# Centring on GpSimd and a constant row in place of the bias products, in a thirty-step recurrence

## What is computed

```python
def step(h, _):
    h = h + 0.01 * jnp.tanh(h)
    h = h * jax.nn.sigmoid(h)
    h = _layernorm(h, ln_w, ln_b)
    h = jnp.einsum('bsc,dc->bsd', h, W) + b
    return (h, None)
x, _ = jax.lax.scan(step, x, None, length=N_ITERS)   # N_ITERS = 30
...
x = x + _L1_ffn_ref(_layernorm(x, axis=-1), L1_ffn_ln_w, L1_ffn_ln_b, L1_ffn_W, L1_ffn_b)
```

## Time and profile before

| | us |
|---|---|
| median of 3 runs | 1304.41 (1303.4 to 1305.09) |
| the profiled execution's own time | 1303.05 |
| its span, first to last instruction | 1301.1 |
| PE, DVE, ACT, POOL busy | 1269.5, 1163.0, 961.4, 755.8 |
| granted TensorE clock, mean | 0.997 |

### The profile page before, as it was taken

One profiled execution on the slowest core, in us unless ns is written; L12 is line 12 of the kernel. 1 busy time (PEld: TensorE's weight loads), 2 busy tenths in 40 slices (PEclk: granted clock), 3 DMA queues, 4 the chain that ended last, 5 costly groups with the idle time before them and its releaser, 6 DMA issues.

```text
span 1301.1 us, 30193 instructions
## 1 busy us (share of the span) xinstructions
PE 1269.5 (98%) x9788; PEld 1150.9 (88%) x9788; DVE 1163.0 (89%) x3032; ACT 961.4 (74%) x1169; POOL 755.8 (58%) x787
## 2 busy tenths in 40 slices
PE   8899999999999999699999999999999999999998
PEld 7677777777777777599999999999999999999998
DVE  7888888888888877899999999999999999999996
ACT  2455555555555555799999999999999999999994
POOL 3455555455555554666666666666666666666664
PEclk9999999999999999899999999999999999999999
DMA  6111111111111000000000000000000000000004
GB/s 191 41 42 46 58 55 44 40 40 40 40 40 40 0 1 1 1 2 1 0 0 0 0 0 0 0 0 0 0 0 0 0 0 0 0 0 0 0 0 129
DMA packets 29810, 27.74 MB, mean 21 GB/s; under 512 B 3285, under 2 KB 21464, under 8 KB 29656
## 3 DMA queue, kind: packets, MB, share of 16 engines
q1 hardware_dynamic: 29784, 27.41, 6.6%
HBM read 23.21 MB, written 4.19 MB: 21 GB/s over the span
## 4 chain that ended last, share of the span: by engine, by line
PE 83%; DVE 10%; ACT 3%; issue 2%; POOL 0%; DMA 0%; SPq 0%; DVEq 0%; ACTq 0%
PE psum L867 33%; PE psum L909 16%; PE psum L884 8%; PE psum L652 4%; PE psum L654 4%; PE psum L653 4%; PE psum L823 4%; PE psum L674 3%; PE psum L669 3%; DVE emb_n L1465 2%; DVE xh_mem L1253 1%; PE psum L663 1%; ACT emb_f L1017 1%; PE psum L683 1%; DVE upd L1431 1%
## 5 line engine op out<-in xcount | busy, mean ns | idle before, releaser
L511 POOL TENSOR_TENSOR h_ring<-g_ring,f_rs 128x512 f32<-128x512 f32 x480 | 485.9, 1043 | 256.7 <-DVE f_rs L1358 256.6
L867 PE MATMUL psum<-w_t,y_all 128*128 128x128 f32 x3840 | 467.6, 275 | 0.0
L867 PEld LDWEIGHTS psum<-w_t,y_all 128*128 128x128 f32 x3840 | 448.0, 192 | 0.0
L1270 DVE BATCH_NORM_STATS2 f_stat<-g_ring 128x6 f32<-128x256 f32 x960 | 393.3, 423 | 2.4 <-ACT g_ring L966 2.4
L909 PE MATMUL psum<-ident,h_ring 128*128 128x128 f32 x1920 | 359.5, 273 | 3.2 <-POOL h_ring L511 2.8
L1287 DVE SCALAR_TENSOR_TENSOR u_ring<-t_ring,psum 128x1024 f32<-128x1024 f32 x232 | 283.3, 1221 | 32.3 <-ACT t_ring L976 27.7
L976 ACT ACTIVATE t_ring<-psum 128x1024 f32<-128x1024 f32 x232 | 238.0, 1026 | 53.7 <-PE psum L867 49.6
L909 PEld LDWEIGHTS psum<-ident,h_ring 128*128 128x128 f32 x1920 | 251.4, 142 | 15.8 <-POOL h_ring L511 3.6
L884 PE MATMUL psum<-bias,ones_bf 65*128 65x256 bf16 x960 | 262.1, 274 | 1.1 <-DVE u_ring L1287 1.1
L980 ACT ACTIVATE y_all<-psum 128x1024 f32<-128x1024 f32 x240 | 243.6, 1015 | 14.6 <-PE psum L909 14.6
L966 ACT ACTIVATE g_ring<-u_ring 128x1024 f32<-128x1024 f32 x240 | 251.6, 1049 | 1.9 <-DVE u_ring L1287 1.6
(11 more groups left out here) (191 smaller groups left out, 1990.5 us busy)
## 6 DMA issues: line engine op xcount, KB each, us to landing
work<-in_adj_dram SPq DMA_DIRECT2D x16, 1024.0 KB, 5.4
x_tok<-in_x_dram SPq DMA_DIRECT2D x16, 256.0 KB, 5.6
out_dram<-y_all SPq DMA_DIRECT2D x7, 512.0 KB, 3.2
work<-in_L_gnn_conv_w_dram SPq DMA_DIRECT2D x1, 1088.0 KB
out_dram<-y_all SPq DMA_DIRECT2D x2, 256.0 KB, 3.3
work<-in_L_gnn_w_ih_dram SPq DMA_DIRECT2D x1, 384.0 KB
work<-in_L_gnn_w_hh_dram SPq DMA_DIRECT2D x1, 192.0 KB
work<-in_L_gnn_W_dram SPq DMA_DIRECT2D x1, 64.0 KB, 5.2
```

The lines of the kernel that those rows point to most:

```text
L511: pool.tensor_tensor(tiles(h_ring[j % 4])[:, NT * h:NT * h + NT, :], tiles(g_ring[j])[:, NT * h:NT * h + NT, :], spread(f_rs[:, both(j), a ...
L867: m = pe.matmul(y_ps[k % 2][:, h, C * t:C * t + C], y_all[:, GT * k + NT * h + t, :], w1_t[:], start=False, stop=True, skip_group_check=True)
L1270: ins = dve.bn_stats(f_stat[:, j % 4, 0, 2 * q:2 * q + 2, :].rearrange("p t w -> p (t w)"), two)
```

## The change

The turned tiles get 127 rows of channels and a last row that holds 1, and the product's weight gets the bias in that row. For this the tiles have to be centred (their channels then sum to zero, so the last channel can be expressed by the others), which POOL does in the instruction that scales.

- POOL: `scale` issues eight tensor-scalars of 128x128 for a group in place of two multiplies of 128x512, each adding `f_less` (minus the mean) and multiplying by `f_rs`. `less_mean` makes `f_less` for two groups in one tensor-scalar of 128x16, in every second slot, after the statistics of both (`f_bn`), and announces it by `f_mean`, for which `scale` waits.
- PE: no `bias` and `bias_free`. The product starts its own accumulation (`start=(t == 0)`), and now waits at its start for the sum that frees `y_ps`. The turns write 127 partitions. `ones_row` fills each of the three banks of `g_ps` with 1, once, before its first turns; the turns leave the last partition alone, so its 1 stays.
- DVE: `split_bias` goes, with 17 instructions; in `fold` the weight's last column is subtracted from the others and replaced by the folded bias. `f_stat` holds eight groups instead of four.

```diff
+LAG_M = 4
...
+            def less_mean(j, s):
+
+                pool.wait_ge(f_bn, s + 2)
+                settle(pool, s_passed_pool)
+                pool.tensor_scalar(f_less[:, j:j + 2, :], f_stat[:, j:j + 2, 0, :, 1], -1.0, 1.0,
+                                   ALU.mult, ALU.mult).then_inc(f_mean, 1)
+
             def scale(i, j, s):
...
+                pool.wait_ge(f_mean, i * (GROUPS // 2) + j // 2 + 1)
                 wait(pool, f_turn, s - 3)
+                settle(pool, s_passed_pool)
                 for h in (j % 2, 1 - j % 2):
-                    at = GT * (j % 2) + NT * h
-                    pool.tensor_tensor(tiles(h_ring[j % 4])[:, NT * h:NT * h + NT, :], tiles(g_ring[j])[:, NT * h:NT * h + NT, :],
-                                       spread(f_rs[:, both(j), at:at + NT], NT, C), ALU.mult).then_inc(f_norm, 1)
+                    for t in range(NT * h, NT * h + NT):
+                        at = GT * (j % 2) + t
+                        ins = pool.tensor_scalar(tiles(h_ring[j % 4])[:, t, :], tiles(g_ring[j])[:, t, :],
+                                                 f_less[:, j, t:t + 1], f_rs[:, both(j), at:at + 1], ALU.add, ALU.mult)
+                    ins.then_inc(f_norm, 1)
...
             def product_group(it, k):
                 s = (it - 1) * GROUPS + k
                 pe.wait_ge(f_state, s + 1)
+                if ends(it, 1) and k < 2:
+                    pe.wait_ge(s_x3, B)
+                elif ends(it, ITERS) and k > 1:
+                    pe.wait_ge(f_out, k - 1)
+                else:
+                    pe.wait_ge(f_u, s + GROUPS - 1)
                 for h in range(2):
                     for t in range(NT):
-                        m = pe.matmul(y_ps[k % 2][:, h, C * t:C * t + C], y_all[:, GT * k + NT * h + t, :], w1_t[:],
-                                      start=False, stop=True, skip_group_check=True)
+                        m = pe.matmul(y_ps[k % 2][:, h, C * t:C * t + C], y_all[:, GT * k + NT * h + t, :], w1c_t[:],
+                                      start=(t == 0), stop=True, skip_group_check=True)
...
-            def bias(k, part):
-                h, c = part // 2, part % 2
-                pe.matmul(y_ps[(k + 1) % 2][:, h, 2 * C * c:2 * C * c + 2 * C], ones_bf[:],
-                          bias1[:, 0:2, :].rearrange("p t c -> p (t c)"),
-                          start=(c == 0), stop=False, skip_group_check=True)
+            def ones_row(b):
+
+                pe.matmul(bank[b], ones_bf[:], first_one[:], start=True, stop=True, skip_group_check=True)
...
-                        m = pe.transpose(g_ps[j % 2][:, t // NT, P * (t % NT):P * (t % NT) + P],
-                                         tiles(h_ring[j % 4])[:, t, :], ident[:])
...
+                    m = pe.transpose(g_ps[j % 2][0:P - 1, t // NT, P * (t % NT):P * (t % NT) + P],
+                                     tiles(h_ring[j % 4])[:, t, 0:P - 1], ident[:])
...
-                for r in range(3):
-                    dve.tensor_copy(b1_cols[:, 32 * r:32 * r + 1], vec(FB1))
+                link(dve.tensor_copy(vec(BF), w1_nat[:, C - 1:C]))
+                dve.tensor_scalar(w1_nat[:, 0:C - 1], w1_nat[:, 0:C - 1], vec(BF), None, ALU.subtract)
+                dve.tensor_copy(w1_nat[:, C - 1:C], vec(FB1))
...
-            def split_bias():
...
-                if isinstance(b, int) and b == 0:
-                    split_bias()
```

More of the change, by code:

```diff
@@ L102, in build @@
         y_all = sb("y_all", [P, B * NT, C])
-        w1_t = sb("w1_t", [P, C])
+        w1c_t = sb("w1c_t", [P, C])
         ident = sb("ident", [P, P])
         ones_bf = sb("ones_bf", [KB, P], BF16)
-        bias1 = sb("bias1", [KB, NT, C], BF16)
+        first_one = sb("first_one", [KB, N], BF16)
         half_neg = sb("half_neg", [P, 8])
-        f_stat = sb("f_stat", [P, 4, 2, GT, 3])
+        f_stat = sb("f_stat", [P, GROUPS, 2, GT, 3])
         f_var = sb("f_var", [P, BY_POWER, GT])
         f_rs = sb("f_rs", [P, 2, PAIR])
+        f_less = sb("f_less", [P, GROUPS, GT])
         f_share = sb("f_share", [P, PAIR])
@@ L297, in build @@
         f_bn = sem("f_bn")
+        f_mean = sem("f_mean")
         f_v = sem("f_v")
@@ L507, in scale @@
                     pool.wait_ge(f_root, pairs(i, j) + 1)
+                pool.wait_ge(f_mean, i * (GROUPS // 2) + j // 2 + 1)
                 wait(pool, f_turn, s - 3)
+                settle(pool, s_passed_pool)
                 for h in (j % 2, 1 - j % 2):
-                    at = GT * (j % 2) + NT * h
-                    pool.tensor_tensor(tiles(h_ring[j % 4])[:, NT * h:NT * h + NT, :], tiles(g_ring[j])[:, NT * h:NT * h + NT, :],
-                                       spread(f_rs[:, both(j), at:at + NT], NT, C), ALU.mult).then_inc(f_norm, 1)
+                    for t in range(NT * h, NT * h + NT):
[3 more added lines that the diff above has]
+                    ins.then_inc(f_norm, 1)
             def slot(it, k):
+                older = earlier(it, k, LAG_M)
+                if older is not None and k % 2 == 0:
+                    less_mean(*older[1:])
                 before = earlier(it, k, LAG_P)
@@ L561, in step @@
                     power(3)
+                    less_mean(2, 2)
                 if l1:
@@ L573, in step @@
                     power(0)
+                    less_mean(0, 0)
                     scale(0, 0, 0)
@@ L608, in spread_vectors @@
                 pe.wait_ge(s_folded1, 1)
-                pe.matmul(bank[TURN_A][0:KB, 0:C], b1_cols, ident[:], start=True, stop=True)
                 for j in range(8):
@@ L891, in slot @@
                 before = earlier(it, k, LAG_T)
[L892 to L899, removed]
-                for n in range(GT):
[L901 to L908, removed]
-                        m = pe.transpose(g_ps[j % 2][:, t // NT, P * (t % NT):P * (t % NT) + P],
-                                         tiles(h_ring[j % 4])[:, t, :], ident[:])
[L911 to L916, removed]
+                if before is None:
+                    return
+                i, j, s = before
+                if ends(i, 0) and j == 0:
+                    pe.wait_ge(s_conv_pre, B)
+                    ones_row(CONV)
+                    pe.wait_ge(s_x_nmp_lo, B)
+                    ones_row(CHAN)
+                elif ends(i, 0) and j == 1:
+                    pe.wait_ge(s_r, B)
+                    ones_row(DIST_A)
+                else:
+                    pe.wait_ge(f_state, s - 1)
+                pe.wait_ge(f_norm, 2 * s + 1)
+                for n in range(GT):
+                    if n == NT:
+                        pe.wait_ge(f_norm, 2 * s + 2)
+                        wait(pe, f_state, s)
+                    t = (n + NT * (j % 2)) % GT
+                    m = pe.transpose(g_ps[j % 2][0:P - 1, t // NT, P * (t % NT):P * (t % NT) + P],
+                                     tiles(h_ring[j % 4])[:, t, 0:P - 1], ident[:])
+                m.then_inc(f_turn, 1)
             slots(pe, slot, LAG_T, 2)
@@ L942, in weights_high @@
                 act.wait_ge(s_wturn, FILLS)
-                act.activation(w1_t[:], bank[CONV + (FILLS - 1) % 4][:, 0:C], ACT.Copy)
+                act.activation(w1c_t[:], bank[CONV + (FILLS - 1) % 4][:, 0:C], ACT.Copy)
                 act.activation(w_full[:, MSG, :], bank[CONV + (FILLS - 1) % 4][:, C:2 * C], ACT.Copy).then_inc(s_whigh, 1)
@@ L1269, in statistics_of @@
                 two = g_ring[j][:, 2 * C * q:2 * C * q + 2 * C].rearrange("p (o c) -> p c o", o=2)
-                ins = dve.bn_stats(f_stat[:, j % 4, 0, 2 * q:2 * q + 2, :].rearrange("p t w -> p (t w)"), two)
+                ins = dve.bn_stats(f_stat[:, j, 0, 2 * q:2 * q + 2, :].rearrange("p t w -> p (t w)"), two)
                 if q == GT // 2 - 1:
@@ L1308, in variance @@
                 dve.wait_ge(f_bn, j + 1)
-                squares = f_stat[:, j % 4, :, :, 2].rearrange("p o t -> p t o")
+                squares = f_stat[:, j, :, :, 2].rearrange("p o t -> p t o")
                 dve.tensor_reduce(f_var[:, j, :], squares, AX_X, ALU.add).then_inc(f_v, 1)
@@ L1338, in root_link @@
                         dve.wait_ge(s_z, B)
-                    squares = f_stat[:, j % 4:j % 4 + 2, :, :, 2].rearrange("p g o t -> p g t o")
+                    squares = f_stat[:, j:j + 2, :, :, 2].rearrange("p g o t -> p g t o")
                     dve.tensor_reduce(root[:, VAR, :].rearrange("p (g t) -> p g t", t=GT), squares, AX_X, ALU.add).then_inc(f_link, 1)
```

26 lines of the change are left out of this document (4 added, 22 removed).

## The result

The changed kernel is slower: 1404.07 us median of four runs (1403.82 to 1404.85) against 1303.91 for the kernel before on the same chip, a ratio of 1.0768 with a 95% interval of 1.075 to 1.0787. The forecast was 1267 us, with a range up to 1335.

What follows compares the result with a forecast made beforehand. PE was taken to bound the kernel at 3.110 us a slot, DVE next at 2.968. Loop -32.9, setup -1.3, loop start +0.5, last eight slots -3.0 sum to -36.7: 1266.3, as median 1267 us; range 1258 to 1335.

Steps and rivals of the forecast that it cites:

- PE's part: PE in the loop: without four bias records a slot takes 24 x 0.111 = 2.67 us, 0.44 less.
- the moved wait: PE, wait for the sum of the group before last, now ahead of the product: priced at 0 us.
- DVE binds next: Steady loop: DVE at 2.968 us stops PE's gain, 0.142 us a slot over 232 slots, 32.9 us.
- POOL's price: POOL's scaling: 0.30 us a tensor-scalar of 128x128, 5.0 us a pair of groups, which fits in 5.94.
- upper bound of 0.42: POOL's 128x128 tensor-scalar: at most 0.42 us start to start, from multiplies with two full inputs at 2.2 ns an element.
- The rival that POOL becomes the bound: POOL between f_root and f_norm: at 0.41 us a piece, slot 3.38 us, +64 us, 1366 us; chance 0.20.
- "In time": POOL's halves before PE's turns: each ready in time, the tightest by 0.2 us, with 0.30 us of PE idle behind.
- Setup: Before the loop: bias splitting goes, so at most PE's 1.34 us wait for emb_n goes, -1.3 us.
- Start of the loop: PE's wait for POOL's first half: four pieces, the small instruction and DVE's two-input sums cost +0.5 us.
- Last eight slots: End of the loop, PE sets the pace: eight times 0.44 is 3.5 us, taken as 3.0 saved.
- The port: Between DVE and POOL: contention taken as 0 in the loop, since DVE's inputs there include at most one from SBUF.
- The clock: PE's granted clock: under 1.00 would show the prediction wrong; 10% of short gaps were expected.

Runs made afterwards that it cites:

- the wide tensor-scalar: The changed kernel with one POOL tensor-scalar of 128x512 with two constants in place of four pieces of 128x128; 1253.26 us.
- the mixed kernels: Against the kernel before, POOL centres at most four tiles of a group; the others keep one multiply and bias products; 1274.60 to 1291.62 us.
- the run of 1686 us: The changed kernel, its tensor-scalars with one operation and one factor from memory (multiply by f_rs), mean not subtracted; 1686.28 us.

## Why the prediction was wrong, step by step

- **PE's part: right.** 24 records a slot at 0.111 us, turns of 127 columns included, as the rows of the wide tensor-scalar (1253 us) show. That the moved wait costs nothing is shown down to DVE's slot of 2.91 us, by that run and the one without bias products (1254 us), and no further.
- **DVE binds next: right, its size a little off.** The step took DVE's busy time of the kernel before, 2.968 us a slot, and allowed for some 0.03 of stalls in it. With the tanh ready in time it is 0.08 less, 2.888, and the slot 2.910. Where no wait is left, DVE's sum starts before its last statistics end (901.66 against 900.98 + 0.77 = 901.75 in the rows of the run without bias products), and its mean length is 1208 ns instead of 1221. The forecast of 1267 for a POOL that keeps up was 13 us too high.
- **POOL's price: the step that failed.** 0.30 us was assumed, 0.431 measured, above even the upper bound of 0.42. The slope behind it was right (the affine select over the small tensor-scalar gives (292 - 184) / 124 = 0.87 ns an element; 0.88 and 0.92 measured). Wrong was the fixed part: I took the length of one lone instruction, 292 ns, as if successive ones overlapped by 0.04 us. In a stream the next begins 0.065 us after the end: 0.362 in place of 0.25. The factors from memory then add 0.07, where 0.05 was allowed. The 0.04 came from long multiplies, and didn't hold for short pieces.
- **The rival that POOL becomes the bound: the mechanism and its formula were right.** 8 x 0.431 + 0.1 = 3.55 us a slot, 3.533 measured, and +0.44 x 236 = 104 in place of the prediction's 64 makes its 1366 into 1406. Its chance, 0.20, was too small, and the range stopped at a piece of 0.39, short of the forecast's own upper bound of 0.42.
- **"In time" was checked for 0.30 us only,** with a slack of 0.2 us at the second half of the first group. The run without bias products shows turns that wait for POOL's old multiplies already, and the mixed kernels lose time by such waits before POOL's sum binds.
- **The ends.** *Setup:* PE's wait for emb_n is gone as forecast, but of its 1.34 us only 0.63 arrive: the first product starts at 545.78 instead of 546.41. *Start of the loop:* forecast +0.5. PE now waits far longer than the 2.85 us of the earlier trace rows:

```profile
549.42 0.71 POOL L507 TENSOR_SCALAR f_less<-f_stat 128x16 f32<-128x16 f32 x1
550.33 4.60 POOL L521 TENSOR_SCALAR h_ring<-g_ring,f_less,f_rs 128x128 f32<-128x128 f32 x8 [0.20 <-issue]
553.34 1.19 PE L921 MATMUL psum<-ident,h_ring 128*127 128x128 f32 x4 [5.61 <-POOL h_ring L521]
```

  The third product starts 2.2 us later than before (559.93 against 557.72), 2.8 more than the setup alone would give. One piece alone holds POOL back by 1.1: it starts at 551.20, the next at 552.75, 1.55 us apart instead of 0.43, while DVE makes a sum whose inputs both lie in SBUF (`t_ring` and `y_all`). The forecast had named such sums, as a small part of its +0.5:

```profile
551.20 1.56 POOL L521 TENSOR_SCALAR h_ring<-g_ring,f_less,f_rs 128x128 f32<-128x128 f32 x1
551.32 1.20 DVE L1284 SCALAR_TENSOR_TENSOR u_ring<-t_ring,y_all 128x1024 f32<-128x1024 f32 x1
552.75 0.45 POOL L521 TENSOR_SCALAR h_ring<-g_ring,f_less,f_rs 128x128 f32<-128x128 f32 x1
```

  *Last eight slots:* nothing was saved; but for the last one, products stay 3.45 to 3.63 us apart, since POOL feeds them too. From the third product to the last the loop is 99.3 us longer (1396.2 - 559.93 against 1294.69 - 557.72), which with 2.2 at its start and 0.5 behind it makes up the 102.0 of the two spans.
- **The port** between DVE and POOL played no part in the steady loop (for its start see above): DVE's statistics keep their length, mean 424 ns beside a POOL that is always busy, against a median of 423 in the earlier trace rows. The clock stayed at 1.00 although PE idles 16% of the steady stretch in short gaps.

## What to carry to other kernels

Price many small instructions by the spacing of a stream of them, not by the length of one: on POOL most of a short tensor-scalar is its fixed part. An engine with slack may take work up to the point where its latency, not its sum, fills the loop it stands in; then work goes where the slack in time is, here into the second group of a pair, and part of a change can win (2.3%) where the whole loses 7.7%. Busy time that an engine shows while it now and then waits can be a little above what it needs.

## What was not expected of the hardware

- A tensor-scalar on POOL of 128x128 float32, from start to start: 0.362 us with two constants, 0.349 with one factor from memory and a constant, 0.431 with two factors, and 0.58 with one factor and no second operation. Why the simplest form is the slowest stays open.
- The same stream of pieces is shown with lengths of 490 and of 902 ns at nearly one spacing (0.431 and 0.428 us). What makes the difference was not tried.
- In the changed kernel, a piece of 0.43 us took 1.55 when DVE's 1.20 us sum with both inputs in SBUF began 0.12 us after it. In the steady loop, where DVE's sum reads one input from PSUM, no piece is longer than 0.525.
- The granted clock was 1.00 with PE idle for 16% of the stretch, and 0.95 in the run of 1686 us, where PE was idle for 29% (424.58 of 600 us busy).
- The busy time of an engine that waits now and then is no exact floor: DVE's fell from 2.968 to 2.888 us a slot when its waits went.
